# Householder steps: the row of e is made before the norm and the coefficients, and VectorE works on it amid the scalar chain

## The reference, cut to what matters

```python
deg = jnp.sum(A, axis=0) + jnp.sum(A, axis=1) - jnp.diagonal(A)
d_inv_sqrt = jnp.where(deg > 0, jax.lax.rsqrt(deg), 0.0)
L_norm = d_inv_sqrt[:, None] * (jnp.diag(deg) - A) * d_inv_sqrt[None, :]
_, U = jnp.linalg.eigh(L_norm)
agg = jnp.einsum('mn,bnd->bmd', U.T, features)
```

## Time and profile before

| what | value |
|---|---|
| median of three runs | 6369.11 us |
| profiled execution, its own device time | 6370.36 us |
| span of the profiled execution, first to last instruction | 6368.6 us |
| busy PE / PEld / DVE / ACT | 4002.2 / 2741.1 / 4479.3 / 1270.0 us |
| mean granted TensorE clock, share of full speed | 0.641 |
| ACT root waiting for PE norm (n of 3 and 4 / n of 1 and 2) | 737.1 us in 248 waits / 534.8 us in 246 waits |
| PE totals waiting for DVE pp (n > 1 / n = 1) | 469.1 us in 384 waits / 195.3 us in 126 waits |

### The profile page before, as it was taken

How to read it: one execution, slowest core, us unless ns; L and a number is a source line. 1 busy time by engine, 2 the same in 40 slices (tenths; PEclk the granted TensorE clock), 3 DMA queues, 4 the chain that set the end, 5 groups by cost and what they waited for, 6 DMA issues and landing times. The chain is left out here.

```text
span 6368.6 us, 81910 instructions
## 1 busy us (share of the span) xinstructions
PE 4002.2 (63%) x23728; PEld 2741.1 (43%) x23728; DVE 4479.3 (70%) x24648; ACT 1270.0 (20%) x3608; POOL 16.8 (0%) x30
## 2 busy tenths in 40 slices
PE   5777766666666655553333333358788699995684
PEld 5667665555555555551000000023342465553352
DVE  6777777777787877778999999941223777724457
ACT  1111211111122222222222222212432111110100
POOL 0000000000000000000000000000000000000000
PEclk9855555555555555555555555569899599997876
DMA  1000000000000000000000000000000000000000
GB/s 34 2 2 2 2 1 1 1 1 1 1 1 1 1 1 1 1 1 0 0 0 0 0 0 0 0 21 0 0 0 0 0 0 0 0 0 0 0 1 27
DMA packets 14096, 17.20 MB, mean 3 GB/s; under 512 B 624, under 2 KB 10000, under 8 KB 13712
## 3 DMA queue, kind: packets, MB, share of 16 engines
q1 hardware_dynamic: 10896, 9.44, 0.5%
q10 hardware_dynamic: 2352, 2.69, 0.2%
q0 software_dynamic: 464, 0.55, 0.0%
HBM read 8.47 MB, written 4.19 MB: 2 GB/s over the span
## 5 line engine op out<-in xcount | busy, mean ns | idle before, releaser
L497 PE MATMUL coef<-vwv 128*128 128x40 f32 (+28 forms) x2476 | 665.7, 396 | 199.2 <-DVE x_parts L422 199.2
L497 PEld LDWEIGHTS coef<-vwv 128*128 128x128 f32 x2476 | 600.2, 326 | 213.3 <-issue 213.3
L792 DVE SCALAR_TENSOR_TENSOR poly<-poly,off,term 128x60 f32<-128x60 f32 x2560 | 609.5, 274 | 0.0
L784 DVE SCALAR_TENSOR_TENSOR term<-cut,rows,poly 128x60 f32<-128x60 f32 x2560 | 597.6, 275 | 9.8
L715 PE MATMUL both_signs<-signs,identb 128*128 128x480 bf16 x320 | 186.2, 582 | 564.8 <-PEq L65 564.8
L554 PE MATMUL totals<-pp_sum,ones 128*128 128x2 f32 x768 | 225.3, 363 | 469.1 <-DVE pp_sum L408 469.1
L1003 PE MATMUL horner_ps<-horner,S 128*128 128x512 f32 x1024 | 460.6, 592 | 0.0
L554 PEld LDWEIGHTS totals<-pp_sum,ones 128*128 128x128 f32 x768 | 192.3, 311 | 508.0 <-DVE pp_sum L408 508.0
L515 PEld LDWEIGHTS product<-x_parts,A_parts 128*128 128x128 bf16 x11136 | 379.0, 109 | 43.0 <-DVE A_parts L338 42.7
L515 PE MATMUL product<-x_parts,A_parts 128*128 128x3 bf16 x11136 | 359.3, 167 | 41.7 <-DVE A_parts L338 41.7
L1523 PE MATMUL gate_ps<-h_sb,wih_t 128*128 x504 | 314.1, 783 | 81.9 <-PEq L65 81.9
(11 more groups left out here) (481 smaller groups left out, 7810.5 us busy)
## 6 DMA issues: line engine op xcount, KB each, us to landing
out_dram<-x_sb SPq DMA_DIRECT2D x4, 1024.0 KB, 7.3
adj_sb<-adj_dram SPq DMA_DIRECT2D x1, 1024.0 KB, 5.6
alpha<-L_gnn_alpha_train_dram POOLq DMA_DIRECT2D x1, 256.0 KB, 5.8
edge_row<-L_gnn_src_dram POOLq DMA_DIRECT2D x1, 128.0 KB, 5.7
edge_row<-L_gnn_dst_dram POOLq DMA_DIRECT2D x1, 128.0 KB, 6.2
w<-L_gnn_Wg_dram ACTq DMA_DIRECT2D x2, 64.0 KB, 4.7
w<-L_gnn_W_dram ACTq DMA_DIRECT2D x2, 64.0 KB, 4.1
x_sb<-x_dram SPq DMA_DIRECT2D x4, 0.5 KB, 10.4
```

Source lines behind the costliest of these rows:

```text
L497: last = pe.matmul(coef[:, 0:2 * j].rearrange("p (j t) -> p j t", t=2), vwv[:, c, j % 2, 1:2].broadcast_to([P, P]), vwv[:, c, 2:2 + j, 1:3 ...
L784: pair(dve.scalar_tensor_tensor(out=term[:, way, :], in0=flat, scalar=rows[:, way, row:row + 1], in1=poly[:, b, way, s + 1, :], op0=ALU.su ...
L792: pair(dve.scalar_tensor_tensor(out=poly[:, b, way, s + 2, :], in0=poly[:, b, way, s, :], scalar=off2[:, way, row:row + 1], in1=term[:, wa ...
```

## The change

TensorE's order is now the same in every stage but for the place of `coefs`: for n of 3 and 4 `row_of`, `norm`, all of `coefs`, `products`; for n of 1 and 2 `norm`, `row_of`, `products`, `coefs`. On VectorE `prod_e` moves from after `x_scaled` to just after `sgn`, `ae` to between `q2` and `nb`, and `prod` from after `inv_mask` to before it. No operation is added or removed.

```diff
                 mark(dve.tensor_scalar(sgn, alpha, 0.0, 0.5, ALU.is_ge, ALU.subtract), "sgn")
+                if j:
+                    dve.wait_ge(row_ready, row - row // NB)
+                    mark(scaled(prod_e[:, c0:C, 1:1 + 2 * j], row_e[:, 0:2 * j]), "prod_e")
                 after("q")
                 mark(dve.scalar_tensor_tensor(out=q2, in0=q, scalar=s, in1=root[:], op0=ALU.mult, op1=ALU.add), "q2")
-                if j == 0:
+                if j:
+                    after("prod_e")
+                else:
                     dve.wait_ge(panel_kept, row // NB)
+                mark(dve.tensor_reduce(ae, prod_e[:, c0:C, 0:1 + 2 * j], AX.X, ALU.add), "ae", row)
                 after("q2")
                 mark(dve.tensor_tensor(nb, q2, sgn, ALU.mult), "nb")
...
                 mark(dve.reciprocal(tau, h), "tau", row)
+                if j:
+                    dve.wait_ge(coef_ready, row - row // NB)
+                    mark(scaled(prod[:, c0:C, 0:2 * j], coef[:, 0:2 * j]), "prod")
                 after("inv_nb")
                 mark(dve.tensor_scalar(inv_mask[:, c0:C], mask, inv_nb, None, ALU.mult), "inv_mask")
                 if j:
-                    dve.wait_ge(coef_ready, row - row // NB)
-                    mark(scaled(prod[:, c0:C, 0:2 * j], coef[:, 0:2 * j]), "prod")
                     after("prod")
                     mark(dve.tensor_reduce(corr, prod[:, c0:C, 0:2 * j], AX.X, ALU.add), "corr")
...
-                if j:
-                    dve.wait_ge(row_ready, row - row // NB)
-                    mark(scaled(prod_e[:, c0:C, 1:1 + 2 * j], row_e[:, 0:2 * j]), "prod_e")
-                    after("prod_e")
-                mark(dve.tensor_reduce(ae, prod_e[:, c0:C, 0:1 + 2 * j], AX.X, ALU.add), "ae", row)
-                if j == 0:
-                    after("corr")
+                after("corr")
                 mark(dve.tensor_tensor(to_y[:, c0:C], corr, inv_mask[:, c0:C], ALU.mult), "to_y")
-                after("ae", row)
                 mark(dve.scalar_tensor_tensor(out=side[:, c0:C], in0=ae, scalar=nb, in1=corr, op0=ALU.mult, op1=ALU.add), "to_side")
...
-                        if j == 0:
-                            pe.wait_ge(dve_did, pos["split", p] if n > 1 else pos["changed", p, C - 1])
-                        elif n > 1:
-                            pe.wait_ge(dve_did, pos["x2", row])
-                        products(c0)
                     if j:
                         pe.wait_ge(dve_did, pos["w", row - 1])
-                    if j and n >= 3:
-                        coefs(row, j, c0, c0)
-                        pe.wait_ge(dve_did, pos["xx", row])
-                    if n >= 3:
-                        norm(j, c0)
-                    if j:
-                        for c in range(c0 + (n >= 3), C):
-                            coefs(row, j, c0, c)
                         row_of(row, j, c0)
                     if n >= 3:
-                        pe.wait_ge(dve_did, pos["x2", row] if j else pos["split", p])
-                        products(c0)
+                        if j:
+                            pe.wait_ge(dve_did, pos["xx", row])
+                        norm(j, c0)
+                        if j:
+                            coefs(j, c0)
+                    if j == 0:
+                        pe.wait_ge(dve_did, pos["split", p] if n > 1 else pos["changed", p, C - 1])
+                    elif n > 1:
+                        pe.wait_ge(dve_did, pos["x2", row])
+                    products(c0)
+                    if j and n <= 2:
+                        coefs(j, c0)
```

More of the change, by code:

```diff
@@ L494, in norm, with coefs @@
                 last.then_inc(norm_ready, 1)
[L496 to L500, removed]
+            def coefs(j, c0):
+                for c in range(c0, C):
+                    last = pe.matmul(coef[:, 0:2 * j].rearrange("p (j t) -> p j t", t=2), vwv[:, c, j % 2, 1:2].broadcast_to([P, P]),
+                                     vwv[:, c, 2:2 + j, 1:3], start=(c == c0), stop=(c == C - 1))
+                last.then_inc(coef_ready, 1)
             def row_of(row, j, c0):
```

## The result

The changed kernel takes 6185.84 us (median of four runs, 6185.08 to 6186.9) against 6368.67 us (the kernel before, four runs too, one more than in its own table above): ratio 0.9714, 95% interval 0.9697 to 0.9731. That is 182.8 us less. The forecast was 154 us less, 6215 us, with a range from 6195 to 6245.

What follows compares the result with a forecast made beforehand. The prediction took the Householder steps to be bound by a loop of waits, not a full engine. Gains of 57 + 22 + 24 + 49 + 2 = 154 us gave 6215 us, range 6195 to 6245.

Steps and rivals of the forecast that it cites:

- what bounds each stage: Householder steps: a loop of waits, no engine full; each stage's gain depends on when v_y can start after q.
- n=4: Steps with j > 0: products hold v_y, no gain up to j=12, full 0.46 us in the last four; 22 us.
- n=2: Steps with j > 0: prod waits 0.2 us for the coefficients; v_y from 2.55 to 2.35 us, 24 us in all.
- n=3: Steps with j > 0: prod waits for nothing; v_y from 2.69 to 2.22 us after q, 57 us in all.
- n=1: Steps with j > 0: L412 from 2.35 to 1.92 us, gain 0.43 us a step, 49 us together.
- A waited pair so costs 0.11 us more than an unwaited one: VectorE: an operation waiting for the one just ahead starts 0.11 us later; all that reordering can remove there.
- the spacings: VectorE: a start comes 0.08 us before the end of the operation ahead if unwaited, 0.03 us after it if waited.
- with the same durations: VectorE's new chain at n=3, j=16 was worked with each operation lasting as long as before the change.
- the six gaps: VectorE, n=3: q2-nb, prod-corr, prod_e-ae 0.11 us each, sgn-q2 0.06, inv_nb-inv_mask 0.05, ae-to_side about 0.04.
- The rule against it: VectorE: the pipe empties after every operation and a semaphore between two costs nothing, so the new order gains nothing.
- 41 us of room: VectorE pairs not in the trace: one gap kept at the upper end costs 0.11 us in 370 steps, 41 us.
- 10 us for the clock: Stages after the Householder part: TensorE's granted clock may differ when their start shifts; 10 us either way.

Runs made afterwards that it cites:

- single-wait run: The changed kernel with unneeded waits of q2 on prod_e, inv_mask on prod and x_scaled on corr, each replacing the wait that stood there: 6315.0 us, ratio 0.9916.

## Why the prediction fell short

**Right:** what bounds each stage. At n=4 early steps gain nothing and the products take over nearly all the rest; at n=2 prod waits for the coefficients; at n=3 and n=1 VectorE's chain is free. The order of TensorE costs norm nothing against the kernel before. Row_e is there when VectorE wants it at n of 3 and 4, and lets prod_e start at 0.18 at n of 1 and 2 (j=16), 0.05 after its earliest place, as forecast. The n=4 stage came out at its forecast of 22 us, because there the products and not VectorE's spacings set the new v_y in all but the last steps of a panel.

**Wrong: the term "A waited pair so costs 0.11 us more than an unwaited one", and the spacings under it.** The mechanism held; the size of this term did not, and neither did "with the same durations". The spacings were read from starts and durations with two decimals, as -0.08 and +0.03. In the trace before, in nanoseconds, they are -84 and +35, so 0.12. The single-wait run shows 36 ns after instead of 84 ns before at three places.

At n=3 (j=18) the six gaps that go then bring: q2 to nb, prod to corr and prod_e to ae 0.12 each, sgn to q2 0.06, inv_nb to inv_mask 0.06, ae to to_side 0.05. Summed in nanoseconds that is 0.54 of the 0.58 us measured. The forecast had 0.48 for the same six. The missing 0.04 lies in operations that last a few nanoseconds less, the four wide ones 20 ns together; why they do is open.

**Why two decimals were enough before and not after.** With the durations of the trace before, the same rounded spacings give v_y of the kernel before within 0.01 us: the waited pairs, each 5 ns too short, and the unwaited ones, most of them 4 to 5 ns too long, cancel. The new chain has one waited pair left and seventeen unwaited ones, and their errors add up. At j=16, still with the durations of before, -0.08 and +0.03 give 2.23, and -84.5 and +35 ns give 2.16; the forecast had 2.22, and 2.10 was measured. So the spacings are 0.07 of the miss, and the shorter operations some 0.05. A sum that fits the old order doesn't show that its terms are right, if the change shifts their mix.

**n=2** adds its own share: 0.29 us a step at j=16 instead of 0.20. The coefficients end 0.05 us earlier than where row_e ended in the earlier trace rows; before, the first product started 0.06 us after its slot was free, for it waited for the last piece of x, and row_of now fills that time. The other 0.04 is the spacing of the chain behind prod (0.88 instead of 0.92 us).

**n=1** had 0.43 us and measured 0.46 at j=18 (L412 at 1.88 instead of 1.92), again the spacings.

**The rule against it.** A semaphore between two VectorE operations was to cost nothing (the Trainium skill, VectorE: DVE Perf Modes, "The DRAIN you can't avoid"). The changed kernel and the single-wait run decide against it for these short operations: the same operations take 183 us less in the new order, and three more waited pairs cost 129 us in 494 steps.

**The range** ended at 6195 because the spacings were given 41 us of room for being larger and 10 us for being smaller. With 10 us for the clock that made 20 below the forecast, and the miss was 29.

## What to carry to other kernels

In a chain of short operations on one engine, put an operation that depends on nothing recent behind each one whose result is waited for: it removes up to 0.12 us per pair here, without removing any work. It pays only if the engine that feeds the moved operation delivers earlier too, for an operation moved forward whose input is late blocks all that stands behind it. Take spacings from starts in nanoseconds or from means over many pairs, and give one operation one wait: a later count on the same semaphore, or an event that implies the others, replaces the rest. In this kernel that was worth 35 us more, and the coefficients ahead of the products 26; both together reach 6132.5 us.

## What the hardware showed beyond that

A second wait in front of a VectorE operation moved its start from 36 ns to 104 to 108 ns after the release, though the first of the two had long been met; on TensorE three waits against one made 115 against 52 ns. The three extra waits on VectorE cost 89 us (6404.3 against 6315.0 us), and dropping two implied ones on TensorE gave 35.
